# Replicated rows of x0 in four bands of 32 partitions instead of two halves of 64

## The reference, cut to what matters

```python
B, F0, D = (1024, 39, 16)
x0 = xk = e                                   # gathered embeddings, [B, 39, 16]
for idx, (W, b) in enumerate([(w0, b0), (w1, b1), (w2, b2)]):   # W: [39, fk, 128], fk = 39, 64, 64
    z = relu(einsum('bhd,bkd,hks->bsd', x0, xk, W) + b[None, :, None])
    if idx != 2:
        xk = z[:, :64, :];  direct.append(z[:, 64:, :])
    else:
        direct.append(z)
logit = sum(concatenate(direct, axis=1), axis=-1)               # [B, 256]
h = relu([logit, dense_ctx] @ W_top1 + b_top1)
h = relu(h @ W_top2 + b_top2);  y = h @ W_top3
```

## Time and profile before

| what | value |
|---|---|
| three runs | 1400.21, 1404.76, 1404.78 us |
| median of the runs | 1404.76 us |
| span of the profiled execution, first to last instruction | 1398.7 us |
| median less span | 6.06 us |
| busy share of the span: PE, DVE, POOL, ACT | 89%, 83%, 65%, 47% |
| mean DMA rate over the span | 168 GB/s |
| loads of `x_rep` | 320 of 512 KB, median 11.2 us from issue to landing |

### The profile page before, as it was taken

How to read it: one execution, slowest core, us unless ns; L and a number is a source line. 1 busy time by engine, 2 the same in 40 slices (tenths; PEclk the granted TensorE clock), 3 DMA queues, 4 the chain that set the end, 5 groups by cost and what they waited for, 6 DMA issues and landing times.

```text
span 1398.7 us, 15290 instructions
## 1 busy us (share of the span) xinstructions
PE 1246.7 (89%) x4128; PEld 771.1 (55%) x4128; DVE 1164.4 (83%) x1054; ACT 653.8 (47%) x757; POOL 908.8 (65%) x581
## 2 busy tenths in 40 slices
PE   0148999997999999999999999999999999999989
PEld 0024666564665666565655666565655566665643
DVE  1128889997999899999989999989999899999850
ACT  1114445553545464555545454555544454454522
POOL 6726777675777767777777677676777644555520
PEclk9978999998999999999999999999999999999999
DMA  6299989988698999989898989999898989899500
GB/s 175 38 171 181 188 178 185 202 178 183 127 185 178 189 186 201 183 176 188 174 188 171 193 177 192 192 187 187 175 186 169 183 186 192 174 195 192 122 0 0
DMA packets 134718, 235.16 MB, mean 168 GB/s; under 512 B 15930, under 2 KB 23083, under 8 KB 134588
## 3 DMA queue, kind: packets, MB, share of 16 engines
q1 hardware_dynamic: 124711, 232.35, 79.9%
q0 software_dynamic: 9984, 2.58, 2.4%
q10 hardware_dynamic: 2, 0.00, 0.0%
HBM read 231.01 MB, written 6.23 MB: 170 GB/s over the span
## 4 chain that ended last, share of the span: by engine, by line
PE 30%; DVE 22%; POOL 17%; issue 14%; DMA 12%; ACT 3%; SPq 1%; DVEq 1%; ACTq 0%; POOLq 0%
PE z_even L709 16%; DVE whole L619 11%; DMA x_rep<-x_rows 9%; POOL gathered L429 9%; PE z_odd L709 8%; POOL rest L441 8%; DVE whole_psum L619 4%; DVE rest L626 4%; ACT head L513 2%; PE z_odd L716 2%; PE whole_psum L787 2%; DVE part L654 1%; DMA x_shift<-x_rows 1%; DMA gathered<-in_tbl,idx 1%; DVE sum L652 1%
## 5 line engine op out<-in xcount | busy, mean ns | idle before, releaser
L441 POOL TENSOR_TENSOR rest<-whole,head 128x1024 fp32r<-128x1024 f32 x256 | 608.7, 2392 | 332.8 <-ACT head L513 324.1
L619 DVE TENSOR_TENSOR whole<-x_bank,x_rep 128x1024 f32<-128x1024 f32 x448 | 534.3, 1213 | 75.2 <-ACT x_bank L501 63.2
L429 POOL DMA_INDIRECT gathered<-in_tbl,idx x312 | 298.2, 956 | 103.8 <-issue 101.1
L513 ACT CAST head<-whole_psum 128x1024 fp32r<-128x1024 f32 x192 | 194.6, 1014 | 354.3 <-DVE whole_psum L619 300.3
L513 ACT CAST head<-whole 128x1024 fp32r<-128x1024 f32 x256 | 268.5, 1049 | 60.9 <-DVE whole L619 30.8
L626 DVE TENSOR_TENSOR rest<-whole_psum,head 128x1024 fp32r<-128x1024 f32 x192 | 234.3, 1220 | 22.1 <-ACT head L513 21.7
L619 DVE TENSOR_TENSOR whole_psum<-x_bank,x_rep 128x1024 f32<-128x1024 f32 x192 | 235.4, 1226 | 19.3 <-DMA x_rep<-x_rows 17.3
L709 PE MATMUL z_odd<-head,w_rest 128*128 128x512 f32 x460 | 207.5, 451 | 28.1 <-POOL rest L441 21.5
L709 PE MATMUL z_even<-head,w_rest 128*128 128x512 f32 x436 | 193.4, 444 | 28.4 <-POOL rest L441 13.6
L709 PE MATMUL z_odd<-whole,w_whole 128*128 128x512 f32 x400 | 189.8, 604 | 13.4 <-DVE whole L619 13.4
L709 PE MATMUL z_odd<-head,w_head 128*128 128x512 f32 x460 | 182.1, 396 | 0.0
(11 more groups left out here) (66 smaller groups left out, 873.7 us busy)
## 6 DMA issues: line engine op xcount, KB each, us to landing
x_rep<-x_rows SPq DMA_DIRECT2D x320, 512.0 KB, 11.2
x_shift<-x_rows SPq DMA_DIRECT2D x96, 546.0 KB
gathered<-in_tbl,idx POOLq DMA_INDIRECT x312
x_rows<-xt SPq DMA_DIRECT2D x32, 78.0 KB
x_rows<-xt SPq DMA_DIRECT2D x32, 40.0 KB
x_rep<-in_W_top SPq DMA_DIRECT2D x2, 512.0 KB, 11.7
w_k<-in_L_rec_w SPq DMA_DIRECT2D x1, 760.5 KB
w_h<-in_L_rec_w SPq DMA_DIRECT2D x1, 760.5 KB
```

The costliest lines, as they stand in the source:

```text
L429: nc.gpsimd.indirect_dma_start(gathered[:, f, :], None, tables[f], bass.IndirectOffsetOnAxis(ap=idx[:, f:f + 1], axis=0)).then_inc(s_gathe ...
L441: nc.gpsimd.tensor_tensor(rest[:, split_slot(product)], whole_slot(product), head[:, split_slot(product)].bitcast(F32), ALU.subtract).then ...
L513: nc.scalar.copy(head[:, split_slot(product)], src).then_inc(s_head, 1)
L619: nc.vector.tensor_tensor(out[0:rows, 0:width, :], xk[0:rows, :].unsqueeze(1).to_broadcast([rows, width, N]), x0, ALU.mult).then_inc(s_pro ...
```

## The change

The two fields of a chunk are spread over four bands of 32 partitions. The even field takes bands 0 and 3 (k = 0 to 31 on partitions 0 to 31, k = 32 to 63 on partitions 96 to 127), the odd field bands 1 and 2 (k = 32 to 63 on partitions 32 to 63, k = 0 to 31 on partitions 64 to 95). The copies of xk in the banks already fit this. A group of `x_rep` is now loaded by three transfers (256 KB to partitions 0 to 31, 512 KB to 32 to 95, 256 KB to 96 to 127). The weights are loaded band by band to match, and their zero padding moves to bands 1 and 2.

```diff
+BAND = P // 4
+BANDS = ((0, 0), (1, BAND), (1, 0), (0, BAND))
+PIECES = (("even", 0, BAND), ("odd", BAND, 3 * BAND), ("even", 3 * BAND, P))
...
-    WEIGHT_LOADS = 11
+    WEIGHT_LOADS = 2 * 6 + 7
...
-            eng.wait_ge(s_rep[rep_place(t, g)], t.visits(2, 32, 32) if g < TWICE else t.count(32, 32))
+            eng.wait_ge(s_rep[rep_place(t, g)], t.visits(2, 48, 48) if g < TWICE else t.count(48, 48))
...
-            sp.wait_ge(s_w12_zero, 2)
+            sp.wait_ge(s_w12_zero, 4)
             for layer, w in ((1, w1), (2, w2)):
                 rows = w.rearrange("h k s -> (h k) s")
-                sp.dma_start(w_loaded[layer][:, 0:CHUNKS - 1, :],
-                             rows[0:whole_rows].rearrange("(c p) s -> p c s", p=P)).then_inc(s_w, 16)
-                sp.dma_start(w_loaded[layer][0:HALF, CHUNKS - 1, :], rows[whole_rows:]).then_inc(s_w, 16)
+                whole_chunks_of_w = rows[0:whole_rows].rearrange("(c p) s -> p c s", p=P)
+                for to, (field, k0) in enumerate(BANDS):
+                    band = slice(BAND * to, BAND * (to + 1))
+                    first = HALF * field + k0
+                    sp.dma_start(w_loaded[layer][band, 0:CHUNKS - 1, :],
+                                 whole_chunks_of_w[first:first + BAND]).then_inc(s_w, 16)
+                    if field == 0:
+                        sp.dma_start(w_loaded[layer][band, CHUNKS - 1, :],
+                                     rows[whole_rows + k0:whole_rows + k0 + BAND]).then_inc(s_w, 16)
...
-                    for half in range(2):
-                        src = source(row, 2 * CPL * g + half, [[0, HALF], [2 * N, CPL], [1, N]])
-                        place = rep_place(nxt, g)
-                        sp.dma_start(x_rep[HALF * half:HALF * (half + 1), place], src).then_inc(s_rep[place], 16)
+                    place = rep_place(nxt, g)
+                    for which, first, end in PIECES:
+                        src = source(row, 2 * CPL * g + (which == "odd"), [[0, end - first], [2 * N, CPL], [1, N]])
+                        sp.dma_start(x_rep[first:end, place], src).then_inc(s_rep[place], 16)
...
-                nc.vector.memset(w[HALF:P, CHUNKS - 1, :], 0.0).then_inc(s_w12_zero, 1)
+                for to in (1, 2):
+                    nc.vector.memset(w[BAND * to:BAND * (to + 1), CHUNKS - 1, :], 0.0).then_inc(s_w12_zero, 1)
```

## The result

The changed kernel took 1409.06 us (median of 20 runs, 1401.43 to 1417.46) and the kernel before 1402.74 us beside it (20 runs, 1397.88 to 1407.05). The medians lie 6.3 us apart; the ratio of the two sets of runs is 1.0054, with a 95% interval of 1.0039 to 1.0068, which is 7.6 us: **slower by 6 to 8 us**, where 9.6 us of gain were forecast. 1409.06 lies outside the range given. One execution of the kernel before that stood beside the last three experiments took 3285 us and is in none of the ratios.

A forecast was written before the change was run, and what follows sets the result against it. PE (96%), DVE (92%) and the DMA engines (share 0.89 of 1.07) were taken as near their end at once. Terms -4.2 - 2.0 - 1.5 - 3.1 + 1.2 = -9.6 us took 1404.76 to 1395.2 us, range 1385 to 1406.

The forecast's parts named there:

- Part 1: Loading a group of `x_rep`: 3.85 us instead of 4.68, saving 0.83 us a group, bounds 0 to 1.67.
- Rival A: `x_rep` loads gain no rate, as the read side limits or only full-width transfers count: 1404.8 to 1406.0 us; chance 0.20.
- Rival D: Slower: outer 32-partition pieces at half rate, a group 1.5 us longer, 1435 us in all; chance 0.05.
- D's sign: Saturated stretches of `x_rep` loads reading under 200 GB/s.
- Part 5: Steady tiles: eight tiles with waits for `x_rep` shorten to 37.25 us each, -3.1 us, bounds 0 to 10.5.
- Rival B: PE and heads have more room, so every wait for `x_rep` is a gain: 19.6 us, 1385.2 us; chance 0.10.
- Part 2: First tile: groups 2, 3 and 4 land 2.49, 3.32 and 4.15 us earlier, gaining 4.2 us, bounds 0 to 8.4.
- Part 3: Second tile: earlier groups 3 and 4 nearly remove DVE's waits, shortening 39.30 us by 2.0, bounds 0 to 3.4.
- Part 4: Third tile: ACT's 1.58 us wait for the last gather shrinks by 1.5 us, bounds 0 to 1.6.
- Part 6: SP: five more transfers a tile, 3 us of issue, hidden in SP's idle time; cost 0.
- Part 7: Weight loads: twelve transfers for four end 2.2 us later, 1.0 us covered; cost 1.2 us, bounds 0 to 3.8.

The follow-up runs named there:

- the last three experiments: The changed kernel with pieces ordered low, high, middle (1398.76 us); with middle, upper, lower (1409.95 us); and with middle first in two-chunk pieces by turns (1393.91 us).
- even half in two: The kernel before, with the even half of each `x_rep` group loaded by two transfers of 32 partitions: 1403.23 us against 1402.69, ratio 0.9998.
- weights only: The changed kernel with its twelve weight transfers, but `x_rep` loaded in halves as before: 1402.90 us against 1402.69 for the kernel before, ratio 1.0002.
- middle first: The changed kernel with each group's pieces issued as partitions 32 to 95, 0 to 31, 96 to 127: 1396.45 us against 1404.99, ratio 0.9935.
- finer halves: The kernel before, with each half of an `x_rep` group in two transfers of two chunks, by turns: 1395.61 us against 1402.09, ratio 0.9943.
- both: The changed kernel with 32 to 95 first and each piece in two of two chunks, by turns, six transfers a group: 1393.91 us against 1403.29, ratio 0.993.
- the transfers alone: Kernels with only SP's `x_rep` transfers in stages of eight groups, nothing computed; the change's three bands made 203 GB/s in the first.
- middle, upper, lower: The changed kernel with each group's pieces issued as partitions 32 to 95, 96 to 127, 0 to 31: 1409.95 us against 1403.29, ratio 1.0056.
- the second kernel of transfers: Only `x_rep` transfers again, 15 stages testing unlike shapes and their order; middle piece first made 249 GB/s, the change's order 215.

## Why the prediction was wrong, step by step

**Part 1 is the step that failed.** It took a group as the sum of pieces priced apart, each at one fixed rate, 2.34 + 1.51 = 3.85 us, and had every group save 0.83 us. In the changed kernel the steady groups took 4.66 us on the mean, as before (4.68), and anything from 3.92 to 5.55. The one fault is a size: the middle piece was priced at 348 GB/s from rows that are all different, and alone, with one repeated row, it made 265, so 1.98 us. The outer pieces' 2.34 was right (226 GB/s gives 2.32). That leaves 4.30 us, still 0.37 better than before. The other fault is the sum itself: in the order low, middle, high the mixture did not keep to its parts, and this took the rest of the saving away. Fast groups near 3.9 us did come; they were not the rule.

**What was left out is the spread.** Parts 2 to 5 moved all landings by one and the same amount. With no gain on the mean and a spread of 1.6 us, the tiles with late loads paid in full (up to 41.40 us against 37.52), and those with early loads could not fall below 37.25. A kernel whose loads just arrive in time loses by unevenness alone. The bounds of part 1 went from 0 to 1.67 us of gain, and a loss was left to rival D.

**Rival A was right about the mean rate and not about its cost.** No rate was gained in the steady tiles, yet the time is 1409.06 and not 1404.8 to 1406.0, since A too had the loads come evenly. Its ground for a limit on the read side was met only at full width (287 against 372).

**Rival D had the sign but not the cause.** The full stretch at 196 GB/s is under the 200 that was named as D's sign, yet it is one slow tile, and pieces of 32 cost nothing. D priced a slower group against the DMA engines' mean free time, 6.6 us a tile, so that less than +1.3 us a group would cost nothing. The slowest groups of the change are +0.9 us, and it lost 13.8 us in 25 tiles against the profile of before, 8.5 to 9.6 us against the two other kernels with `x_rep` in halves (even half in two, 1259.17 - 281.86 = 977.31; weights only, 1262.38 - 283.95 = 978.43). Groups 2 to 4 are loaded in one run between the release of their buffers and their use, and there each delay adds up, while the free time lies elsewhere in the tile.

**Parts 2 to 5 hold in part once the loads are faster.** A group of 3.85 us came in no kernel on the mean; the nearest are 4.44 us (middle first), 4.38 (finer halves) and 4.16 (both).
- Part 5, -3.1 us from the steady tiles, with an upper bound of 10.5: from the sixth to the thirty-first tile the finer halves took 1250.41 - 280.22 = 970.19 us, the middle first 971.70, both together 971.49. Against the 973.05 of before that is -2.9, -1.4 and -1.6; against the two other kernels with plain halves (977.31, 978.43) it is 5.6 to 8.2 us. The profile of before was a favourable one, so that the -2.9 meets the forecast is in part luck. The floor of 37.25 us, read from a like tile before, stood in all of them. Rival B is out.
- Part 2, the first tile, -4.2: layer 2 of the first tile to that of the second took 35.93 us before, 32.64 with the middle first (-3.3), 34.77 with finer halves (-1.2) and 30.55 with both (-5.4). But with the middle first layer 2 of the first tile began 2.5 us later (91.27 against 88.74). The second tile's began at 123.91 against 124.67 us, 0.8 earlier, and with both cures at 120.03, 4.6 earlier. The last group of the first tile landed at 114.91 with the middle first, not at 111.5.
- Part 3, the second tile, -2.0: 39.30 us before; 38.46 with finer halves and 38.51 with both (-0.8), 40.11 with the middle first. Too large.
- Part 4, the gathers of the third tile, -1.5: ACT's wait of 1.58 us was 2.09 in the changed kernel, 1.34 with the middle first, 1.24 with finer halves and 0.26 with both. It goes only when much of the load goes.

**Part 6, SP, 0:** right. The last kernel issues fifteen transfers a tile more than the change, and is the fastest.

**Part 7, the weights, +1.2:** of the right size in the trace, not visible in the time. `w_rest` was forecast to end at 59.9 and ended at 59.28 with the weights alone; layer 2's first product came 1.3 us later. In the medians this is within the error (1.0002). The profile of the changed kernel, taken alone, would have told the opposite.

**The sum.** -9.6 us was forecast for the layout. With the order of the pieces changed it gave a ratio of 0.9935, some -9.1 us. That this is so near is luck: its groups take 4.44 us and not 3.85, and its terms do not come as they were added up (layer 2 of the second tile starts 0.8 us earlier where -4.2 was forecast, the second tile 0.8 longer where -2.0 was). The medians show what the order is worth, and no single profile shows where all of the 9 us lie: this kernel's is 3.5 us shorter than that of before.

**What stays open** is why the order counts and why one order gives fast tiles and slow ones. In the transfers alone low-high-mid (213) and mid-low-high (241, 247) are one cycle and yet unlike, and behind `x_shift` the ranking turns. It would fit that the 16 DMA engines drift apart within a piece and then meet at the same side of the written memory, or not, as the next piece has it. They do drift: the last sixteen increments of a group 4 come over 0.8 to 3.4 us. With the middle first and with middle, upper, lower the slow groups are those where this is wide (correlation 0.78 and 0.71 over 25 tiles), but in the changed kernel it is 0.20. The records don't name the engine, and the causes weren't told apart; that repeated rows are needed for the gap speaks for a part of the read side that this picture leaves out. Nor was the odd half issued from ACT's queue tried in the whole kernel.

## What to carry to other kernels

Price a sequence of transfers as a sequence, and ask how even it will be: rates of the pieces measured alone missed the mixture by 17% (244 against 203), and a change of order in one line was worth 1.2%. When transfers are made more even, try all orders of them, and smaller pieces by turns, in the kernel itself. And price a transfer by how late it makes its own user, not by the mean free share of the DMA engines. Take its time from all landings: those that were waited for showed 5.07 us a group where all of them showed 4.66.

## What was not expected of the hardware

- The same 1.049 MB in three pieces on one queue went at 193 to 249 GB/s by the order of the pieces alone, each piece from one repeated row, at a DMA share of 0.96 to 1.01. The share of busy engines says nothing of the rate: a share of 0.84 moved 183 GB/s in the fastest kernel, one of 0.89 moved 182 before.
- A transfer to 128 partitions whose source repeats one row is slower than one with a row for each partition: 287 against 372 GB/s with full engines. At 0 to 63, where the write side caps it, they are 204 and 209. At 32 to 95 they are 265 and 329, but at shares of 0.76 and 0.95, so that a difference over the busy time is not shown.
- The same three transfers a group, in one order and one kernel, took 3.92 to 5.55 us, and both groups of a tile were fast or slow together.
- A single transfer to partitions 32 to 95 made 329 GB/s, and halves issued from two queues 310 and, in the second kernel of transfers, 295, where from one queue they made 214. The Trainium skill, page "SBUF — State Buffer", section "Can I just issue two DMAs to hit both halves?", has it that only a single transfer over all 128 partitions reaches all 16 ports. Both measurements speak against that sentence, which was one ground for rival A. The same page's section "Door 1: The DMA port swizzle" gives about 218 GB/s for one half, and the 204 for 0 to 63 agrees.
- Loads of the weights by bands, rows of 512 bytes, went at 207 GB/s and a share of 1.23 (changed kernel, 20 to 26 us) where 128 partitions at once had 277 and 1.06.
